# Order of DVE's, ScalarE's and TensorE's work in a fused group norm and attention kernel, changed around V and the output

## The chip, the cores and the metric

One core of one Trainium2 chip. The time is device microseconds of one execution; the runs shown are three executions of the whole program.

## What is computed

For each of 16 batch elements x of 512 channels by 1024 pixels (float32):

```
h = group_norm(x, 32 groups) * w + b
q, k, v = split(qkv_w @ h + qkv_b)              # 512 channels each
attn = softmax(q^T k / sqrt(512), over keys)    # 1024 x 1024
out = x + out_w @ (attn @ v^T)^T + out_b
```

## The kernel before, in words

The weights are multiplied together once: G from those of q and k, U from those of v and out. An element then has four stages on TensorE: T = G^T h (8 units, each a tile of 128 x 512 in one of the 8 PSUM banks), the score stage (7 products of half size by a Strassen-like scheme, with 4 tiles each, 28 units), V = h^T U (8 units, one for each tile of 128 keys), and the output (two halves of 512 queries, 4 tiles of 128 channels each, 8 units). Scores are held with keys in partitions.

Every matmul operand is split in a high part (rounded to fp32r by ScalarE) and a low part (what is left, by DVE), and each product is three matmuls: high by high, high by low, low by high (`three`, lines 262 to 264). So a T or V unit has 12 matmuls, a score unit 6 and an output unit 24, all of 512 columns: 96 + 168 + 96 + 192 = 552 per element.

Each engine runs its own written-out list and meets the others through semaphores.

- **TensorE** (lines 402 to 407): `t_units`, `score_products`, `v_units`, `output_units(b, 0)`, `output_units(b, 1)`. `t_bank_free` (308) holds a T unit until the scaled output has been read out of its bank: unit j of the next element waits for scaled tile j of this one. `t_bank_read` (321) holds a score product until what lies in its bank has been read.
- **ScalarE** (524 to 588): high parts of T (`t_direct_part`, `t_sum_part`), copies of scores, exponentials (510), high parts of the probabilities p (517) and of V (522), then the next element's h (425, 421) and the high parts of combined h (430).
- **DVE** (928 to 1029): low parts of T (816) and sums of T units (833, 839), sums of scores (846), the running maximum (858), statistics of the next x (690), subtraction of the maximum (865), low parts of V (875) and p (870), the tree that adds p over keys (881 to 887), the inverse of the sums (894), low part of the next h (724), its four combined sums (739 to 744) and their low parts (748), the key dot (757, 760), and the scaled output tiles (902), for which there are three buffers.
- **GpSimd** (650 to 665): maximum over partitions (631), twice; the group norm's power -1/2 (656); sum over partitions (636), twice; the adds of the scaled tiles into DRAM (645); the reduction of the key dot (623) between those of the two halves.
- **SP** (237 to 252) issues the other DMAs in a fixed order: x out and in, group statistics, then for half 0 the row of sums to DRAM and back in another shape, the inverses to DRAM and back to all partitions, the same for half 1, and the key bias. The transfers of one half are finished before those of the next begin, so the row of half 1 follows the inverses of half 0.

Group statistics (`group_variance`, `group_spread`, `affine_pair`) of element b + 1 are worked out during element b. `h_combined` (727) waits until both rows of sums are in DRAM, since it writes over the tiles they come from.

Of the kernel before, what the change touches and what calls it, by code (L numbers as in the profile page):

```python
# [37 lines left out]
T_SUM = {S1: (1, 2), S2: (3, 5), S3: (4, 6), S4: (7, 8)}  # L38

# [3 lines left out]
def attention_kernel(nc, x, wq, wk, wv, wo_t, cols, block_avg, out):  # L43
# [5 lines left out]
    with ctx:  # L49
# [80 lines left out]
        def t_bank(b, j):  # L130
            return (j + 1) % 8 if b == 0 else j
# [127 lines left out]
        def _(pe):  # L259
# [48 lines left out]
            def t_bank_free(b, j):  # L308
# [3 lines left out]
                elif j < 3:  # L312
                    pe.wait_ge(s_prod_lo[0], CT)
                elif j < 6:
                    pe.wait_ge(s_prod_lo[1], j - 2)
                elif j == 6:
                    pe.wait_ge(s_vec_sb, 3)
                else:
                    pe.wait_ge(s_prod_lo[1], CT)
# [25 lines left out]
            def score_products(b):  # L345
                for p, (a, name) in enumerate(PRODUCTS):
                    own_bank = p in (P_A12, P_S1, P_S4)
                    for i in range(CT):
                        cs = slice(i * P, (i + 1) * P)
                        if i == 0:  # L350
                            pe.wait_ge(s_tlo, b * 14 + 2 * a + 2)
# [36 lines left out]
            def output_units(b, nb):  # L388
                for c in range(CT):
                    cs = slice(c * P, (c + 1) * P)  # L390
                    pe.wait_ge(s_vlo, b * 8 + CT * nb + c + 1)
                    for m in range(MT):
                        if c == 0:
                            if nb == 0:
                                pe.wait_ge(s_vlo, b * 8 + m + 1)
                            pe.wait_ge(s_plo, b * 8 + nb * CT + m // 2 + 1)
                        a = three(ring[:, CT * nb + c, :], v_part(v_hi_all, m)[:, cs], v_part(v_lo_all, m)[:, cs],
                                  p_tiles(r_hi, nb, m)[:, 0, :], p_tiles(r_lo, nb, m)[:, 0, :], m == 0, m == MT - 1)
                    a.then_inc(s_unit, 1)

            v_hi_all, v_lo_all = r_hi, r_lo
# [8 lines left out]
        def _(act):  # L410
# [82 lines left out]

            def copy_scores(b, p, i, m, to, done):

                act.wait_ge(s_unit, b * UNITS + S0 + 4 * p + i + 1)
# [27 lines left out]
            for b in range(B):  # L524
                copy_a21(b, 0)
                copy_a21(b, 1)
                for kk in range(2):
                    t_direct_part(b, A22, kk)
                for kk in range(2):
                    t_sum_part(b, S1, kk)  # L530
                for kk in range(2):
                    t_direct_part(b, A11, kk)
                for a in (S2, S3):
                    for kk in range(2):
                        t_sum_part(b, a, kk)
                for kk in range(2):
                    t_direct_part(b, A12, kk)
                for kk in range(2):
                    t_sum_part(b, S4, kk)
# [514 lines left out]
```

## Time and profile before

| | before |
|---|---|
| median of 3 runs | 2242.78 us (2241.51 to 2244.41) |
| the profiled execution | 2240.99 us, span 2239.2 us |
| busy: PE, DVE, ACT, POOL | 2089.9, 1619.2, 953.3, 415.6 us |
| chain that ended last | PE 68%, DVE 16%, issue 6%, ACT 6%, POOL 2% |
| mean granted clock of TensorE | 0.961 of full speed |

PE is TensorE, ACT is ScalarE, POOL is GpSimd. Matmuls overlap in the records: each shows 0.39 us at full clock, but they start every 0.23 us, so the time between starts is the one to count with. The bracket behind a row gives the idle time of the engine before it and the last thing it waited for. "ring" is the PSUM tensor of 8 banks; "r_hi" and "r_lo" hold parts of T, V, p and combined h; "run_max" and "spare" also serve as buffers of scaled output.

### The profile page before, as it was taken

Reading aid. Unit: us, or ns where it says so; the run is one execution under the profiler, and the core shown is the slowest. Engines: PE = TensorE matmul, PEld = TensorE weight load, DVE = VectorE, ACT = ScalarE, POOL = GpSimd, SP = SyncE. Lnnn points to the kernel's source line nnn. Section 1 sums busy time; section 2 is a strip of 40 time slices with the busy share of each in tenths; the row PEclk is TensorE's granted clock in tenths of the full one; section 3 lists DMA queues with packets and bytes.
Section 4 is the critical chain, followed back from the end, with each engine's and each line's share of the span. In section 5 each row is a group of like instructions: output and inputs, shape, how many; then the busy total and the mean of one; then the engine's idle time right before and its main releaser. Section 6 shows DMA issues by size and latency. Waiting matters only on the chain.

```text
span 2239.2 us, 23037 instructions
## 1 busy us (share of the span) xinstructions
PE 2089.9 (93%) x8956; PEld 1712.7 (76%) x8956; DVE 1619.2 (72%) x1949; ACT 953.3 (43%) x1179; POOL 415.6 (19%) x237
## 2 busy tenths in 40 slices
PE   8789999898998989989899898989989899898998
PEld 6668778686886868868687786878868688686886
DVE  7678677776767678676776867767777776767754
ACT  6353344434444343444433445334453444444341
POOL 2012030211302113030120302203021130211302
PEclk9899999999999999999999999999999999999999
DMA  5204122140321303213031220402214032130303
GB/s 156 77 5 78 42 43 81 16 108 1 48 77 27 98 1 48 77 29 95 1 56 68 38 86 6 96 23 44 81 20 104 1 48 76 29 95 1 48 38 48
DMA packets 88269, 118.37 MB, mean 53 GB/s; under 512 B 47824, under 2 KB 48432, under 8 KB 88160
## 3 DMA queue, kind: packets, MB, share of 16 engines
q0 software_dynamic: 19296, 35.92, 11.4%
q1 hardware_dynamic: 68864, 80.98, 11.0%
q8 instruction: 71, 1.16, 0.2%
q14 instruction: 38, 0.31, 0.0%
HBM read 46.78 MB, written 67.74 MB: 51 GB/s over the span
## 4 chain that ended last, share of the span: by engine, by line
PE 68%; DVE 16%; issue 6%; ACT 6%; POOL 2%; POOLq 0%; DVEq 0%
PE ring L262 23%; PE ring L263 23%; PE ring L264 23%; DVE stage L865 3%; ACT stage L510 3%; DVE r_lo L875 2%; DVE stage L846 2%; DVE run_max L858 2%; DVE r_lo L870 2%; DVE stage L881 2%; ACT r_hi L517 2%; POOL all_max L631 1%; ACT r_hi L522 1%; DVE stage L884 1%; DVE group_mv L908 1%
## 5 line engine op out<-in xcount | busy, mean ns | idle before, releaser
L262 PE MATMUL ring<-r_hi 128*128 128x512 f32 x1568 | 636.5, 406 | 128.7 <-DVE r_lo L875 120.0
L263 PE MATMUL ring<-r_lo,r_hi 128*128 128x512 f32 x1568 | 629.7, 402 | 0.0
L264 PE MATMUL ring<-r_hi,r_lo 128*128 128x512 f32 x1568 | 628.6, 401 | 0.0
L262 PEld LDWEIGHTS ring<-r_hi 128*128 128x128 f32 x1568 | 306.5, 195 | 210.7 <-DVE r_lo L875 137.5
L264 PEld LDWEIGHTS ring<-r_hi,r_lo 128*128 128x128 f32 x1568 | 306.1, 195 | 66.2
L263 PEld LDWEIGHTS ring<-r_lo,r_hi 128*128 128x128 f32 x1568 | 306.9, 196 | 63.0
L510 ACT ACTIVATE stage<-stage 128x1024 f32<-128x1024 f32 x128 | 135.5, 1058 | 450.3 <-DVE stage L865 448.5
L497 ACT ACTIVATE stage<-ring,keybias 128x512 f32<-128x512 f32 x256 | 173.0, 688 | 248.7 <-PE ring L264 248.7
L631 POOL PARTITION_ALL_REDUCE all_max<-run_max x32 | 57.2, 1787 | 943.8 <-DVE run_max L858 668.7
L846 DVE TENSOR_TENSOR stage<-stage,ring 128x512 f32<-128x512 f32 x192 | 131.5, 685 | 115.4 <-PE ring L264 62.6
L262 PE MATMUL ring<-h_hi,g_hi 128*128 128x512 f32 x512 | 199.4, 389 | 0.0
L264 PE MATMUL ring<-h_hi,g_lo 128*128 128x512 f32 x512 | 199.2, 389 | 0.0
L264 PE MATMUL ring<-u_hi,h_lo 128*128 128x512 f32 x512 | 199.2, 389 | 0.0
L263 PE MATMUL ring<-h_lo,g_hi 128*128 128x512 f32 x512 | 199.2, 389 | 0.0
L263 PE MATMUL ring<-u_lo,h_hi 128*128 128x512 f32 x512 | 199.2, 389 | 0.0
L262 PE MATMUL ring<-u_hi,h_hi 128*128 128x512 f32 x512 | 199.2, 389 | 0.0
L636 POOL PARTITION_ALL_REDUCE stage<-stage x32 | 129.8, 4056 | 340.6 <-DVE stage L887 180.7
L865 DVE TENSOR_TENSOR stage<-stage,all_max 128x1024 f32<-128x1024 f32 x128 | 183.3, 1451 | 0.0
L875 DVE TENSOR_TENSOR r_lo<-ring,r_hi 128x512 fp32r<-128x512 f32 x128 | 86.6, 687 | 116.8 <-ACT r_hi L522 116.8
L870 DVE TENSOR_TENSOR r_lo<-stage,r_hi 128x1024 fp32r<-128x1024 f32 x128 | 155.9, 1218 | 16.7 <-ACT r_hi L517 16.7
L858 DVE TENSOR_TENSOR run_max<-run_max,stage 128x512 f32<-128x512 f32 x192 | 137.8, 722 | 36.4 <-ACT stage L497 32.0
L262 PE MATMUL ring<-h_hi,r_hi 128*128 128x512 f32 x384 | 150.3, 391 | 14.7 <-DVE stage L833 14.7
(100 smaller groups left out, 3012.5 us busy)
## 6 DMA issues: line engine op xcount, KB each, us to landing
xs<-x_in SPq DMA_DIRECT2D x64, 512.0 KB, 6.0
out<-xs SPq DMA_DIRECT2D x64, 512.0 KB, 3.2
out<-run_max POOLq DMA_DIRECT2D x86, 256.0 KB, 4.3
out<-spare POOLq DMA_DIRECT2D x42, 256.0 KB, 4.5
inv<-inv_row SPq DMA_DIRECT2D x32, 256.0 KB, 3.8
stage<-stage POOLq DMA_DIRECT2D x3, 512.0 KB, 8.5
stage<-wk SPq DMA_DIRECT2D x4, 256.0 KB, 4.0
stage<-wq SPq DMA_DIRECT2D x4, 256.0 KB, 5.1
```

Source lines behind the costliest of these rows:

```text
L262: nc.tensor.matmul(ps_out, st_hi, m_hi, start=first, stop=False, skip_group_check=goes_on)
L263: nc.tensor.matmul(ps_out, st_hi, m_lo, start=False, stop=False, skip_group_check=goes_on)
L264: return nc.tensor.matmul(ps_out, st_lo, m_hi, start=False, stop=last, skip_group_check=goes_on)
L497: nc.scalar.activation(stage[:, to, :], ring[:, i, :], ACT.Identity, bias=keybias[:, m:m + 1]).then_inc(done, 1)
L510: nc.scalar.activation(here, here, ACT.Exp, scale=SCALE).then_inc(s_exp, 1)
L631: nc.gpsimd.partition_all_reduce(all_max[:, :], run_max[nb][:, :], P, bass.bass_isa.ReduceOp.max).then_inc(s_allmax, 1)
L636: nc.gpsimd.partition_all_reduce(stage[:, 8 * nb + 1, :], stage[:, 8 * nb, :], P, bass.bass_isa.ReduceOp.add).then_inc(s_allsum, 1)
L846: nc.vector.tensor_tensor(stage[:, to, :], stage[:, to, :], ring[:, CT + i, :], ALU.add).then_inc(done, 1)
L858: nc.vector.tensor_tensor(run_max[nb][:, :], first, stage[:, 8 * nb + m, :], ALU.max).then_inc(s_rmax[nb], 1)
L865: nc.vector.tensor_tensor(here, here, all_max[:, :].rearrange("p (o n) -> p o n", o=1).to_broadcast([P, 2, HALF]), ALU.subtract).then_inc( ...
L870: nc.vector.tensor_tensor(p_tiles(r_lo, nb, 2 * q, 2), stage[:, 8 * nb + 2 * q:8 * nb + 2 * q + 2, :], p_tiles(r_hi, nb, 2 * q, 2).bitcast ...
L875: nc.vector.tensor_tensor(v_part(r_lo, m), ring[:, m, :], v_part(r_hi, m).bitcast(FP32), ALU.subtract).then_inc(s_vlo, 1)
```

## The change

- Output: `output_units` walks over key tiles outside and the four channel tiles inside, so that the four banks of a half fill together (but for the last half of the last element, which keeps the old order). V's low part m and the pair m // 2 of p are waited for at each key tile.
- T and scores: ScalarE and DVE split A22 and A11 first, then A12, and the sums S1 to S4 last; `T_SPLIT` holds the new counts that TensorE waits for. The first copies of scores don't add the key bias; `add_first` on DVE adds it, and the key bias is computed later.
- Around V: group variance before the S4 sums; V's low parts 5 to 7 and the subtractions of half 1 ahead of the group spread and of the sum tree of half 0; low parts of h, combined h, key dot and scaled tiles in new places.
- First element: other banks for T units 3 to 7, the low parts of combined h before the key dot, another order of splits.

```diff
+T_SPLIT = {A22: 0, A11: 2, A12: 4, S1: 6, S2: 8, S3: 10, S4: 12}
...
         def t_bank(b, j):
-            return (j + 1) % 8 if b == 0 else j
+            return (1, 2, 3, 4, 0, 5, 6, 7)[j] if b == 0 else j
...
-                elif j < 6:
-                    pe.wait_ge(s_prod_lo[1], j - 2)
-                elif j == 6:
+                elif j < 7:
+                    pe.wait_ge(s_prod_lo[1], (1, CT, 2, 3)[j - 3])
+                else:
                     pe.wait_ge(s_vec_sb, 3)
-                else:
-                    pe.wait_ge(s_prod_lo[1], CT)
...
-                            pe.wait_ge(s_tlo, b * 14 + 2 * a + 2)
+                            pe.wait_ge(s_tlo, b * 14 + T_SPLIT[a] + 2)
...
             def output_units(b, nb):
-                for c in range(CT):
+                by_keys = (b, nb) != (B - 1, NB - 1)
+                steps = [(c, m) for m in range(MT) for c in range(CT)]
+                if not by_keys:
+                    steps.sort()
+                for c, m in steps:
                     cs = slice(c * P, (c + 1) * P)
-                    pe.wait_ge(s_vlo, b * 8 + CT * nb + c + 1)
-                    for m in range(MT):
-                        if c == 0:
-                            if nb == 0:
-                                pe.wait_ge(s_vlo, b * 8 + m + 1)
-                            pe.wait_ge(s_plo, b * 8 + nb * CT + m // 2 + 1)
...
-                    a.then_inc(s_unit, 1)
+                    if m == 0 and (c == 0 or nb == 0):
+                        pe.wait_ge(s_vlo, b * 8 + CT * nb + c + 1)
+                    if c == 0:
+                        pe.wait_ge(s_vlo, b * 8 + m + 1)
+                        pe.wait_ge(s_plo, b * 8 + nb * CT + m // 2 + 1)
+                    a = three(...)
+                    if m == MT - 1:
+                        a.then_inc(s_unit, 1)
...
# ScalarE
+            def copy_first(b, i):
+                act.wait_ge(s_bias_out, (b + 1) * DMA)
+                act.wait_ge(s_unit, b * UNITS + S0 + 4 * P_A11 + i + 1)
+                nc.scalar.activation(stage[:, i, :], ring[:, i, :], ACT.Identity).then_inc(s_p1, 1)
...
-                copy_a21(b, 0)
-                copy_a21(b, 1)
+                if b > 0:
+                    for kk in range(2):
+                        copy_a21(b, kk)
+                for a in (A22, A11):
+                    for kk in range(2):
+                        t_direct_part(b, a, kk)
+                if b == 0:
+                    for kk in range(2):
+                        copy_a21(b, kk)
                 for kk in range(2):
-                    t_direct_part(b, A22, kk)
-                for kk in range(2):
-                    t_sum_part(b, S1, kk)
-                for kk in range(2):
-                    t_direct_part(b, A11, kk)
-                for a in (S2, S3):
+                    t_direct_part(b, A12, kk)
+                for a in (S1, S2, S3, S4):
                     for kk in range(2):
                         t_sum_part(b, a, kk)
-                for kk in range(2):
-                    t_direct_part(b, A12, kk)
-                for kk in range(2):
-                    t_sum_part(b, S4, kk)
-                act.wait_ge(s_kb, b + 1)
                 for i in range(CT):
-                    copy_scores(b, P_A11, i, i, i, s_p1)
+                    copy_first(b, i)
...
-                exponential(b, 1, 0)
-                p_part(b, 1, 0)
-                v_hi_part(b, 6)
-                v_hi_part(b, 7)
-                for q in range(1, CT):
+                for q in range(2):
                     exponential(b, 1, q)
                     p_part(b, 1, q)
+                v_hi_part(b, 6)
+                exponential(b, 1, 2)
+                p_part(b, 1, 2)
+                v_hi_part(b, 7)
+                exponential(b, 1, 3)
+                p_part(b, 1, 3)
...
# DVE
             h_combined(0)
+            for c in range(CT):
+                h_combined_rest(0, c)
...
-            for c in range(CT):
-                h_combined_rest(0, c)
-            dve.wait_ge(s_bqk, 1)
...
+            def add_first(b, i):
+                if i == 0:
+                    dve.wait_ge(s_kb, b + 1)
+                dve.wait_ge(s_p1, b * 4 + i + 1)
+                dve.wait_ge(s_unit, b * UNITS + S0 + 4 * P_A12 + i + 1)
+                nc.vector.scalar_tensor_tensor(stage[:, i, :], ring[:, CT + i, :], keybias[:, i:i + 1], stage[:, i, :],
+                                               ALU.add, ALU.add).then_inc(s_c11, 1)
...
+                if b == 0:
+                    for a in (A22, A11):
+                        for kk in range(2):
+                            t_direct_rest(b, a, kk)
                 for kk in range(2):
-                    t_direct_rest(b, A22, kk)
+                    if b > 0:
+                        t_direct_rest(b, A22, kk)
                     t_sum(b, S1, kk)
                 if b > 0:
                     scale_output(b - 1, 1, 3)
                 for kk in range(2):
-                    t_sum_rest(b, S1, kk)
-                for kk in range(2):
-                    t_direct_rest(b, A11, kk)
+                    if b > 0:
+                        t_direct_rest(b, A11, kk)
                     t_sum(b, S2, kk)
                     t_sum(b, S3, kk)
-                for a in (S2, S3):
-                    for kk in range(2):
-                        t_sum_rest(b, a, kk)
-                key_bias(b)
                 for kk in range(2):
                     t_direct_rest(b, A12, kk)
                     t_sum(b, S4, kk)
-                for kk in range(2):
-                    t_sum_rest(b, S4, kk)
-
+                for a in (S1, S2, S3, S4):
+                    for kk in range(2):
+                        t_sum_rest(b, a, kk)
+                key_bias(b)
                 for i in range(CT):
-                    add_scores(b, P_A12, i, i, s_p1, s_c11)
+                    add_first(b, i)
...
+                if more:
+                    group_variance(b + 1)
                 for i in range(CT):
                     add_scores(b, P_S4, i, 8 + i, s_p2, s_c12)
...
                 v_rest(b, 4)
+                subtract_max(b, 1, 0)
+                subtract_max(b, 1, 1)
+                v_rest(b, 5)
+                subtract_max(b, 1, 2)
+                subtract_max(b, 1, 3)
+                v_rest(b, 6)
+                p_rest(b, 1, 0)
+                v_rest(b, 7)
                 if more:
                     group_spread(b + 1)
                 sum_tree(b, 0)
-                v_rest(b, 5)
-                subtract_max(b, 1, 0)
-                subtract_max(b, 1, 1)
-                v_rest(b, 6)
-                v_rest(b, 7)
+                p_rest(b, 1, 1)
+                p_rest(b, 1, 2)
+                p_rest(b, 1, 3)
                 if more:
                     affine_pair(b + 1)
-                p_rest(b, 1, 0)
-                subtract_max(b, 1, 2)
-                p_rest(b, 1, 1)
-                subtract_max(b, 1, 3)
-                p_rest(b, 1, 2)
-                p_rest(b, 1, 3)
                 sum_tree(b, 1)
+
+                if more:
+                    for k in range(CT - 1):
+                        h_rest(b + 1, k)
                 inverse(b, 0)
-
                 if more:
-                    h_rest(b + 1, 0)
-                scale_output(b, 0, 0)
-                if more:
-                    h_rest(b + 1, 1)
-                scale_output(b, 0, 1)
-                if more:
-                    h_rest(b + 1, 2)
                     h_rest(b + 1, 3)
-                scale_output(b, 0, 2)
+                    h_combined(b + 1)
+                for c in range(CT):
+                    scale_output(b, 0, c)
                 inverse(b, 1)
-                if more:
-                    h_combined(b + 1)
-                scale_output(b, 0, 3)
                 if more:
                     for k in range(CT):
                         key_dot(b + 1, k)
-                scale_output(b, 1, 0)
-                if more:
-                    h_combined_rest(b + 1, 0)
-                    h_combined_rest(b + 1, 1)
-                scale_output(b, 1, 1)
-                if more:
-                    h_combined_rest(b + 1, 2)
-                    h_combined_rest(b + 1, 3)
-                scale_output(b, 1, 2)
+                    for c in range(CT):
+                        h_combined_rest(b + 1, c)
+                for c in range(CT - 1):
+                    scale_output(b, 1, c)
```

The wait of `copy_scores` for the key bias moved into the function, and `key_bias(0)` now waits for the dot of the two biases itself.

## Rows read from the trace of the kernel before

**Rows 1.** Who waited for whom on TensorE: total us, times, longest.

```profile
PE ring L262 <- DVE r_lo L875: 120.0, 31, 5.3
```

**Rows 2.** TensorE in order of time: start us, us, line, operation, idle before.

```profile
73.39 0.77 PE L262 MATMUL ring<-h_hi,r_hi 128*128 128x512 f32 x1 [14.68 <-DVE stage L833]
...
900.00 0.39 PE L262 MATMUL ring<-h_hi,r_hi 128*128 128x512 f32 x1
...
944.20 0.39 PE L262 MATMUL ring<-u_hi,h_hi 128*128 128x512 f32 x1
...
1097.91 0.80 PE L262 MATMUL ring<-r_hi 128*128 128x512 f32 x1 [4.63 <-DVE r_lo L875]
...
2232.89 0.39 PE L264 MATMUL ring<-r_hi,r_lo 128*128 128x512 f32 x1
```

**Rows 3.** Stretches: us, busy (x) by engine, granted clock, DMA, GB/s.

```profile
1093.30:1096.90 3.60, 0.00 (x0) 0.00 (x0) 3.53 (x3) 0.00 (x0) 0.00 (x0) 1.00 0.09 2
1097.40:1107.60 10.20, 6.81 (x15) 4.93 (x16) 8.57 (x10) 5.09 (x6) 4.15 (x1) 0.50 0.01 2
```

**Rows 4.** DVE in order of time, around V and the output.

```profile
1070.92 2.34 DVE L865 TENSOR_TENSOR stage<-stage,all_max 128x1024 f32<-128x1024 f32 x2
...
1088.39 0.68 DVE L875 TENSOR_TENSOR r_lo<-ring,r_hi 128x512 fp32r<-128x512 f32 x1
1092.84 0.17 DVE L916 COPY group_pair<-group_mv 32x16 f32<-32x16 f32 x1 [3.77 <-POOL group_rstd L656]
...
1097.18 0.68 DVE L875 TENSOR_TENSOR r_lo<-ring,r_hi 128x512 fp32r<-128x512 f32 x1
```

**Rows 5.** ScalarE in order of time: one exponential and the next.

```profile
1099.03 1.06 ACT L510 ACTIVATE stage<-stage 128x1024 f32<-128x1024 f32 x1 [11.73 <-DVE stage L865]
...
1102.03 1.06 ACT L510 ACTIVATE stage<-stage 128x1024 f32<-128x1024 f32 x1
```

**Rows 6.** GpSimd in order of time.

```profile
1092.22 0.59 POOL L656 TENSOR_TENSOR group_rstd<-group_veps,minus_half 32x1 f32<-32x1 f32 x1 [7.04 <-issue]
1103.45 4.24 POOL L636 PARTITION_ALL_REDUCE stage<-stage  x1 [10.64 <-issue]
```

**Rows 7.** DVE in order of time, beside reductions of GpSimd.

```profile
51.13 8.96 DVE L748 TENSOR_TENSOR r_lo<-stage,r_hi 128x1024 fp32r<-128x1024 f32 x4
...
1104.49 3.26 DVE L865 TENSOR_TENSOR stage<-stage,all_max 128x1024 f32<-128x1024 f32 x1
```

**Rows 8.** SP's queue in order of time: the DMAs it issued.

```profile
981.79 0.34 SPq L230 DMA_DIRECT2D inv_row<-own_inv  x1
983.24 0.32 SPq L235 DMA_DIRECT2D inv<-inv_row  x1
985.99 0.24 SPq L224 DMA_DIRECT2D sum_row<-stage  x1
987.15 0.32 SPq L226 DMA_DIRECT2D own_sum<-sum_row  x1
```

**Rows 9.** DVE in order of time: next h, scaled tiles; last, the page's DMA line.

```profile
987.23 0.69 DVE L902 TENSOR_TENSOR run_max<-ring,inv 128x512 f32<-128x512 f32 x1 [4.36 <-DMA inv<-inv_row]
...
997.18 0.68 DVE L902 TENSOR_TENSOR run_max<-ring,inv 128x512 f32<-128x512 f32 x1
...
1002.40 0.68 DVE L902 TENSOR_TENSOR run_max<-ring,inv 128x512 f32<-128x512 f32 x1
...
2209.53 1.29 DVE L902 TENSOR_TENSOR run_max<-ring,inv 128x512 f32<-128x512 f32 x2 [5.58 <-DMA inv<-inv_row]
...
2215.93 0.69 DVE L902 TENSOR_TENSOR run_max<-ring,inv 128x512 f32<-128x512 f32 x1 [4.43 <-DMA out<-run_max]
...
out<-run_max POOLq DMA_DIRECT2D x86, 256.0 KB, 4.3
```

**Rows 10.** DVE in order of time, in the first element.

```profile
44.70 1.22 DVE L744 TENSOR_TENSOR stage<-stage 128x1024 f32<-128x1024 f32 x1
...
64.69 1.40 DVE L833 SCALAR_TENSOR_TENSOR stage<-ring,t_bias,stage 128x512 f32<-128x512 f32 x2
```

## What the change was predicted to do

> **What bounds the kernel now.** I read first who waits for whom on TensorE, then TensorE in order of time, the granted clock by stretches, and last the other engines in one period. TensorE waits in one place only: 31 waits, 120.0 us in all, for a low part of V [rows 1]. Elsewhere it issues a 512-column matmul every 0.2267 us (195 steps, 900.00 to 944.20) [rows 2]. An element of the batch has 552 of them (96 for T, 168 scores, 96 V, 192 output), 125.1 us; by the sum below it costs 11.2 us more.
>
> I count from A, the start of the output stage. The stalled matmul starts at 1097.91; its forerunner started 4.63 + 0.39 earlier, at 1092.89 [rows 2], and is the last of five key tiles (15 matmuls), so A = 1089.72. Here output tile 0 walks through eight key tiles in 5.4 us, and DVE can't keep up: it stood 3.77 us until the group's root arrived, and then ran the spread and sum tree (4.3 us, 1092.84 to 1097.18) ahead of V's part 5 [rows 4]. With 31 waits in 16 elements there is a second one for the parts behind it. The idle also halves the clock: 1.00 through 1093.3 to 1096.9, then 0.50, the 1.2 GHz level, for 10.2 us [rows 3]. Both waits and the slow stretch make up the 11.2 us.
>
> **Part 1, output by key tiles.** Now all four tiles advance with the key tile, 12 matmuls or 2.72 us each, so V part m is due at A + 2.72 m, and probabilities' pair q at A + 5.44 q. Part 7 is due at A + 19.0 instead of A + 4.8. The matmuls and weight loads are as many as before; only banks alternate every three matmuls. The score products in the 195 steps change banks every six matmuls, some 20 times, and the mean step doesn't show it to 0.1 us in all, so a change costs under 0.005. I take 0 (bounds: 0 and 0.5 us for the 112 changes more of an element).
>
> **Part 2, DVE and ScalarE around A.** The group variance (about 1.1 us) goes ahead of the S4 sums, where DVE waits for TensorE, so the subtractions, at A - 18.8 before [rows 4], start 0.4 us earlier. V's part 4, A - 1.3 before, starts at A - 1.8. From start to start an operation on 1024 columns takes 1.14 us and one on 512 takes 0.60, a little less than the records of 1.22 and 0.68 (the two subtractions of rows 4 take 2.34, one record more than one step). Two subtractions, part 5, two subtractions end at A + 4.0. ScalarE gets its first subtraction at A + 0.05; an exponential, a copy and two V copies take 3.0 us together [rows 5], so V's high part 7 comes at A + 6.7, its low part at A + 7.3 to 7.9. It is due at 19.0: **the old stall is gone**, with 11 us to spare. All p parts of half 1, due from A + 21.8, are also in time (below).
>
> **Part 3, what is late next.** Everything pushed behind V now stands in one DVE queue up to the first scaled tile of half 1, which frees a bank for T unit 4 of the next element: due at A + 43.52 + 4 x 2.72 = A + 54.4. Step by step:
> - Group spread 0.16, sum tree of half 0 4.18: A + 12.2. Three low parts of p, 3.4.
> - GpSimd's sum over partitions starts 11.2 us after the root, with no wait that the profile shows (1092.22 to 1103.45), A + 13.3 to 14.0, until about A + 17.9 [rows 6]. An operation of 1024 columns under it took 3.26 instead of 1.21 [rows 7]: +2.05. Affine 0.46, sum tree 4.18: A + 22.35.
> - h low parts 0 to 2: 3 x 1.14, and +2.05 for GpSimd's second sum, which used to run while DVE waited for a DMA: A + 27.8 (28.5 if ScalarE's copies, which wait for the first sum's row in DRAM, are the slower).
> - The inverse of half 0 stands there. The combined h sums wait for the second sum's row in DRAM, and SP sends that only behind the inverse's two transfers: 0.2 to the store, 1.45 to the load, 0.35 to issue it, 1.16 to land [rows 8], so A + 31.0 to 31.7, one to two us later than DVE (h low part 3 done at 29.1 to 29.9). **A new wait.** The four sums take 4.65, 1.14 each and 0.1 for their own order [rows 10]: A + 35.7 to 36.4. The inverses land 4.0 after their issue (983.24 to 987.23) [rows 8, 9], before that.
> - Four scaled tiles now stand together, and there are three buffers. The fourth waits until the first one's add into DRAM has landed. The end of the kernel shows exactly that: 2209.53 to 2215.93, 6.4 us from the first to the fourth [rows 9]. A + 42.1 to 42.8. **The second new wait.** Behind it are queued the other inverse, the key dot and all four low parts of combined h.
> - 0.7 for it and the inverse, 4.6 for the key dot (997.78, behind 997.18, to 1002.40) [rows 9]: A + 47.4 to 48.1. Four low parts under GpSimd's key-dot reduction took 8.96 in the first element, 4.6 alone [rows 7]; it is four again, together: A + 56.3 to 57.0. The scaled tile needs 0.69 more.
>
> So bank 4 is free at A + 57.0 to 57.7, against 54.4: **2.6 to 3.3 us of stall per element, 2.9 taken.** Bounds: with the median landing of such a store, 4.3 us from an issue 1.3 us behind the tile [rows 9], the fourth tile comes 0.8 earlier; with that and one hold of 2.05 fewer the stall is 0.05. One hold more, or the stores slower by as much, makes it 4.5 to 5. I take the middle, since three stores close together are what the end's row has. T units 5 to 7 are served in time: the last scaled tile of half 1 ends at A + 63.9 and is due at A + 65.5.
>
> Would such a stall halve the clock? After 3.6 us of idle the clock was still 1.00 [rows 3]. I take 2.9 us as too short, and the cost of the slow stretch as zero.
>
> **Part 4, T and score stage.** A11's products need two splits ahead of them instead of three; sums' low parts come last. DVE has 8 x 0.6 us of these left when A12's unit is split, ends about S + 7 (S is the start of the score stage), and they are due from S + 10.9. Key bias and first sums follow the product of A12, which they have to wait for. Input shift, its DMAs and the statistics move by under 1 us, and the statistics end before the add at S + 23.8 that was next. Nothing on TensorE's path: 0, with the due times as cover.
>
> **Part 5, start.** In the first element bank 0 was the last one freed, and TensorE stood 14.68 us until 73.39 [rows 2]. Now bank 0 holds T unit 4, and needs the fourth sum only. DVE: combined h done at 44.70 + 1.14, four low parts 4.56, key dot 4.63, bias 0.08: 55.1. Four splits and four sums at 0.66 (two in 1.40) [rows 10]: the fourth sum ends at 60.4, TensorE starts at 60.6. **12.8 us earlier**, and with 2.2 us of idle, without the slow matmuls after it. These eight run beside GpSimd's key-dot reduction; they read PSUM. Bounds: 0, and the 4.4 us that the low parts lost to it [rows 7]. I take 0, since the 1024-column rows that were held all read SBUF alone.
>
> **The sum.** First score matmul 60.6; from it to the end 16 x 552 - 96 = 8736 matmuls x 0.2267 = 1980.2; from the last matmul's slot (2232.89 + 0.23) [rows 2] to the end 6.1, as before; 15 stalls x 2.9 = 43.5. Span 2090.4. The same sum for the kernel before, 73.4 + 1980.2 + 6.1 = 2059.7, leaves 179.5 for 16 stalls with their slow stretches, 11.2 each. The profiled execution took 1.8 more than its span, and the median 1.8 more than that: **2094**, 6.6% less than 2242.8 (2090.4 + 3.6).
>
> **Rivals.**
> - *No new stall* (0.22). DVE reaches bank 4 before A + 54.4 because the stores land faster, or a hold falls between operations. 2046.9 + 3.6 = 2050.5. For: the median landing is shorter than my row. Against: it needs 2.6 us in a chain where I gave no reserve. Between it and mine each us of stall is 15 us.
> - *The clock falls at the new stall* (0.12). A stall over about 3.7 us, or a chip less patient than rows 3 show, makes the matmuls behind it run at 0.50 for 10.2 us, 5.1 us lost: 2094 + 15 x 5.1 = 2170. The Trainium skill ("TensorE: Matmul & The Clock Gate", HAM oscillation) says that a wait in every round can slow the clock every round, which rows 3 agree with for the old stall.
> - *Slower than before* (0.03). Place: the three reductions of GpSimd that DVE's queue in part 3 now meets. If each held DVE until its own end, and PSUM's readers too, the low parts of p would wait from A + 13.4 to A + 17.9 (2.4 us more than I count), h's low part 1 1 us more and combined h's 1.7 more: a stall of 8.0, the clock falls, 5.1 more, and the start loses 4.4: 2046.9 + 4.4 + 15 x 13.1 + 3.6 = 2251. From a stall of 6.1 on the element costs more than the 11.2 before. Against: the operation that began 1.04 us into a reduction of 4.24 lost 2.05, and not the 3.2 that were left of it [rows 6, 7]. The Trainium skill ("SBUF — State Buffer", Who interferes with whom) holds for that case that the later one "fully blocks" until the first is done, if it reads two tensors of SBUF; the length of the hold in rows 7 doesn't agree with it.
> - *It does not do what it says* (0.03): TensorE still stops in the output stage, as DVE's queue has something ahead of V's last parts that I missed: 2242.8, less the start's 12.8 at most.
>
> **How the numbers follow.** Mine (stall 1.5 to 4.5, no slow clock) has 0.60 and spans 2073 to 2118. The range takes it, the first rival below and a little above: 2048 to 2125; outside are the others, 0.18. A measurement of this kernel can tell about 0.2% from no change. Faster: 0.60 + 0.22 + 0.12 = 0.94; same 0.02 and slower 0.04 from the last two, the second of them split.
>
> **What would show it.** TensorE's waits: none for V's low parts; 15 of about 2.9 us, before matmuls that read h and g, for a scaled tile (line of the output scaling). DVE waiting 2 to 4 us for a store of the output, and shortly for a sum's row. A granted clock of 1.00 from the first score matmul on. First score matmul near 60.6. It is wrong if TensorE's waits are absent, fall elsewhere, or carry 0.50 behind them.

## The result and the profile after

The changed kernel takes 2205.4 us (median of 4 runs, 2198.7 to 2214.4) against 2242.2 for the kernel before: ratio 0.984, 95% interval 0.980 to 0.988. It is faster, by 1.6% where 6.6% were forecast, and far outside the range of 2048 to 2125. Its profiled execution took 2198.66 us, with a span of 2196.8.

Who waits for whom on TensorE, in the changed kernel (line numbers of that kernel: 924 is the scaled output tile, 846 a sum of T units; total, times, longest):

```profile
PE ring L263 <- DVE run_max L924: 74.6, 10, 8.3
PE ring L263 <- DVE spare L924: 39.3, 5, 8.4
...
PE ring L263 <- DVE stage L846: 1.9, 1, 1.9
```

The 31 waits for V's low parts [rows 1] are gone, all of them. In their place stand the 15 waits for a scaled tile that the prediction named, but they take 113.9 us: 7.6 each and not 2.9. TensorE in order of time shows both ends of the argument, the start and one stall:

```profile
60.01 0.47 PE L263 MATMUL ring<-h_hi,r_hi 128*128 128x512 f32 x1 [1.88 <-DVE stage L846]
...
1128.15 0.79 PE L263 MATMUL ring<-h_hi,g_hi 128*128 128x512 f32 x1 [7.42 <-DVE run_max L924]
```

The first score matmul starts at 60.0 (60.6 forecast, 73.4 before [rows 2]). With the prediction's own sum, 60.0 + 1980.2 + 6.1 = 2046.3 is the span without stalls, so 150.5 us, 10.0 a stall, go with the 15 stalls. 7.6 of it is waiting; the other 2.4 is, above all, slow matmuls. The stretches around this stall (columns as in [rows 3]):

```profile
1121.00:1123.50 2.50, 0.00 (x0) 0.00 (x0) 2.50 (x1) 0.45 (x1) 2.50 (x1) 1.00 0.14 54
...
1128.10:1131.00 2.90, 2.85 (x7) 2.27 (x8) 2.90 (x5) 0.00 (x0) 2.54 (x3) 0.50 0.60 60
...
1134.00:1139.00 5.00, 5.00 (x23) 4.13 (x22) 4.14 (x7) 1.38 (x2) 0.86 (x1) 1.00 0.66 95
```

The clock is at 1.00 in the first microseconds of the idle, at 0.50 (1.2 GHz) when the matmuls come back, and at 1.00 again some microseconds later, as before the change behind the old stall.

The stalled matmul starts 7.81 after its forerunner, so T unit 4 was due at 1120.57 and, 54.4 earlier, A = 1066.17. DVE from V's last part on, to be held against part 3 of the prediction:

```profile
1073.55 0.69 DVE L897 TENSOR_TENSOR r_lo<-ring,r_hi 128x512 fp32r<-128x512 f32 x1 [0.70 <-ACT r_hi L534]
...
1074.31 2.27 DVE L903 TENSOR_TENSOR stage<-stage 128x2048 f32<-128x2048 f32 x1
...
1077.88 0.69 DVE L909 TENSOR_TENSOR stage<-stage 128x512 f32<-128x512 f32 x1
1078.49 3.48 DVE L892 TENSOR_TENSOR r_lo<-stage,r_hi 128x1024 fp32r<-128x1024 f32 x3
...
1084.68 3.29 DVE L906 TENSOR_TENSOR stage<-stage 128x1024 f32<-128x1024 f32 x1
...
1091.62 1.23 DVE L736 TENSOR_TENSOR h_lo<-stage,h_hi 128x1024 fp32r<-128x1024 f32 x1 [2.93 <-ACT h_hi L426]
...
1097.30 0.17 DVE L916 RECIPROCAL own_inv<-own_sum 128x4 f32<-128x4 f32 x1
...
1103.22 1.23 DVE L751 TENSOR_TENSOR stage<-stage 128x1024 f32<-128x1024 f32 x1 [3.57 <-DMA sum_row<-stage]
...
1107.89 0.68 DVE L924 TENSOR_TENSOR spare<-ring,inv 128x512 f32<-128x512 f32 x1
...
1113.24 0.69 DVE L924 TENSOR_TENSOR spare<-ring,inv 128x512 f32<-128x512 f32 x1 [3.47 <-DMA out<-spare]
...
1118.54 8.96 DVE L760 TENSOR_TENSOR r_lo<-stage,r_hi 128x1024 fp32r<-128x1024 f32 x4
1127.42 1.27 DVE L924 TENSOR_TENSOR run_max<-ring,inv 128x512 f32<-128x512 f32 x2
```

| step, us behind A | forecast | measured |
|---|---|---|
| V's low part 7 starts | 7.3 | 7.4 |
| first sum tree done | 12.2 | 12.4 |
| GpSimd's first sum starts | 13.3 to 14.0 | 18.5 |
| second sum tree done | 22.35 | 22.5 |
| inverse of half 0 | 27.8 to 28.5 | 31.1 |
| combined h starts | 31.0 to 31.7 | 37.05 |
| first scaled tile | 35.7 to 36.4 | 41.7 |
| fourth scaled tile | 42.1 to 42.8 | 47.1 |
| first scaled tile of half 1 | 56.3 to 57.0 | 61.25 |

Both new waits are there, with the 3.57 and 3.47 us in brackets. Both sum trees and all before them are right to 0.2 us, the second one partly by luck: the hold of 2.05 us by GpSimd's sum, forecast on the low parts of p, fell on the second tree (3.29 in its row, for some 1.2). GpSimd's sum is the first step that is off. GpSimd and SP in the same stretch:

```profile
1067.93 1.67 POOL L668 TENSOR_TENSOR group_rstd<-group_veps,minus_half 32x1 f32<-32x1 f32 x1 [6.67 <-issue]
1084.64 3.25 POOL L648 PARTITION_ALL_REDUCE stage<-stage  x1 [15.04 <-DVE stage L903]
1088.90 3.23 POOL L648 PARTITION_ALL_REDUCE stage<-stage  x1 [1.01 <-DVE stage L909]
```

```profile
1097.50 0.34 SPq L231 DMA_DIRECT2D inv_row<-own_inv  x1
1100.10 0.32 SPq L236 DMA_DIRECT2D inv<-inv_row  x1
1100.47 0.29 SPq L225 DMA_DIRECT2D sum_row<-stage  x1
1103.21 0.32 SPq L227 DMA_DIRECT2D own_sum<-sum_row  x1
```

The sum starts 16.7 us after the start of the root, where it was 11.2 before [rows 6]. What both kernels have in common is the sum tree: it ended at 1078.57 here, 6.1 us before the sum starts. Before, the operation ahead of V's part 5 (start 1097.18 [rows 4]) was the tree's last, and the sum followed at 1103.45 [rows 6], 6.2 us after the tree's end. It is so in all of the first 15 elements: 6.0 to 6.4 us from the tree to the sum before, 5.9 to 6.5 after, while from the root it is 11.0 to 11.4 before and 15.9 to 16.8 after. The last element has no root ahead of its sum, as no next x needs one, and already in the kernel before its sum starts 0.2 us after the tree (DVE, then GpSimd):

```profile
2183.37 0.69 DVE L887 TENSOR_TENSOR stage<-stage 128x512 f32<-128x512 f32 x1
```

```profile
2184.26 3.23 POOL L636 PARTITION_ALL_REDUCE stage<-stage  x1 [8.28 <-DVE stage L887]
```

And the store of half 1's row, 0.37 us behind the load of the inverses, took 2.74 us to land instead of 1.16 [rows 8], counted to SP's next issue.

### The profile page after: what moved, and what is told of

It is laid out like the page before. It is cut to its first block, busy times and chain, and to the rows that moved or that the text cites. A ratio compares the mean times of both kernels' runs of the same rounds, so it can differ in the third digit from the quotient of the medians.

```text
span 2196.8 us, 23374 instructions
## 1 busy us (share of the span) xinstructions
PE 2065.0 (94%) x8956; PEld 1700.9 (77%) x8956; DVE 1618.8 (74%) x1949; ACT 935.1 (43%) x1179; POOL 424.3 (19%) x237
## 3 DMA queue, kind: packets, MB, share of 16 engines
q8 instruction: 71, 1.16, 0.2%
## 4 chain that ended last, share of the span: by engine, by line
PE 42%; DVE 27%; ACT 13%; DMA 7%; issue 7%; POOL 2%; SPq 0%; DVEq 0%; ACTq 0%; POOLq 0%
PE ring L263 14%; PE ring L264 14%; PE ring L265 14%; DVE r_lo L892 4%; ACT stage L522 4%; DVE r_lo L760 4%; DVE stage L887 3%; DMA sum_row<-stage 3%; ACT r_hi L529 3%; DVE stage L903 2%; DVE r_lo L897 2%; POOL stage L648 2%; ACT stage L430 2%; ACT h_hi L426 2%; DMA out<-run_max 2%
## 5 line engine op out<-in xcount | busy, mean ns | idle before, releaser
L263 PE MATMUL ring<-r_hi 128*128 128x512 f32 x1568 | 611.6, 390 | 8.1 <-DVE r_lo L690 8.1
L264 PE MATMUL ring<-r_lo,r_hi 128*128 128x512 f32 x1568 | 611.0, 390 | 0.0
L265 PE MATMUL ring<-r_hi,r_lo 128*128 128x512 f32 x1568 | 610.8, 390 | 0.0
L264 PEld LDWEIGHTS ring<-r_lo,r_hi 128*128 128x128 f32 x1568 | 294.9, 188 | 60.9
L263 PE MATMUL ring<-h_hi,g_hi 128*128 128x512 f32 x512 | 214.7, 419 | 113.9 <-DVE run_max L924 74.6
L643 POOL PARTITION_ALL_REDUCE all_max<-run_max x32 | 57.2, 1788 | 920.6 <-DVE run_max L880 651.9
L509 ACT ACTIVATE stage<-ring,keybias 128x512 f32<-128x512 f32 x192 | 132.2, 688 | 227.6 <-PE ring L265 227.6
L263 PEld LDWEIGHTS ring<-h_hi,g_hi 128*128 128x128 f32 x512 | 103.9, 203 | 142.4 <-DVE run_max L924 78.8
L492 ACT ACTIVATE r_hi<-ring,t_bias 128x512 fp32r<-128x512 f32 x96 | 65.1, 690 | 278.0 <-PE ring L265 278.0
L430 ACT ACTIVATE stage<-xs,h_bias,h_scale 128x1024 f32<-128x1024 f32 x62 | 76.5, 1234 | 216.9 <-DMA sum_row<-stage 213.3
L648 POOL PARTITION_ALL_REDUCE stage<-stage x32 | 113.0, 3555 | 256.1 <-DVE stage L903 167.2
L880 DVE TENSOR_TENSOR run_max<-run_max,stage 128x512 f32<-128x512 f32 x192 | 132.5, 695 | 36.4 <-ACT stage L509 32.0
```

Source lines behind the costliest of these rows:

```text
L263: nc.tensor.matmul(ps_out, st_hi, m_hi, start=first, stop=False, skip_group_check=goes_on)
L264: nc.tensor.matmul(ps_out, st_hi, m_lo, start=False, stop=False, skip_group_check=goes_on)
L265: return nc.tensor.matmul(ps_out, st_lo, m_hi, start=False, stop=last, skip_group_check=goes_on)
L430: nc.scalar.activation(h_full[:, k, :], xs[:, k, :], ACT.Identity, bias=h_bias[:, k:k + 1], scale=h_scale[:, k:k + 1]).then_inc(done, 1)
L509: nc.scalar.activation(stage[:, to, :], ring[:, i, :], ACT.Identity, bias=keybias[:, m:m + 1]).then_inc(done, 1)
L648: nc.gpsimd.partition_all_reduce(stage[:, 8 * nb + 1, :], stage[:, 8 * nb, :], P, bass.bass_isa.ReduceOp.add).then_inc(s_allsum, 1)
```

## The experiments

**The output order alone.** The kernel before with only `output_units` exchanged for the new one:

```diff
-                for c in range(CT):
-                    pe.wait_ge(s_vlo, b * 8 + CT * nb + c + 1)
-                    for m in range(MT):
+                by_keys = (b, nb) != (B - 1, NB - 1)
+                steps = [(c, m) for m in range(MT) for c in range(CT)]
+                if not by_keys:
+                    steps.sort()
+                for c, m in steps:
...
```

> The kernel before with the output walked by key tiles and nothing else of the change. Theory (what the output order gains is real, and what costs time in the changed kernel is DVE's new order behind V): the 31 waits for V's low parts vanish; first score matmul stays near 73.4 us; TensorE's next waits are short ones (about 0.6, 1.7 and 1.3 us an element) for scaled tile 3 and for the splits of T, as the old order of T's splits is tight; some 2060 us without them, 2105 us with them, clock near 1.00. Rival (the walk by key tiles itself costs TensorE, through its bank changes or its waits): time near 2200 us, with steps between output matmuls longer than 0.2267 us.

Measured: 2094.9 us, ratio 0.934 (0.933 to 0.936), clock 0.996. TensorE's waits there (908 is the scaled tile, 822 a low part of T, 839 the sum in the first element):

```profile
PE ring L262 <- DVE stage L839: 14.7, 1, 14.7
PE ring L262 <- DVE r_lo L822: 12.0, 15, 0.8
...
PE ring L262 <- DVE run_max L908: 0.8, 4, 0.2
PE ring L262 <- DVE spare L908: 0.6, 3, 0.2
```

This one part brings 6.6%, four times what the whole change brings. The walk by key tiles costs nothing that shows; DVE's old order is just fast enough for it. The time lies between the 2060 and the 2105 of the expectation, as the waits were shorter than I had worked out.

**SP's store of half 1's row first**, in the changed kernel:

```diff
+                send_sums(b, 0)
                 own_sums(b, 0)
+                send_sums(b, 1)
                 spread_inverses(b, 0)
                 own_sums(b, 1)
```

(`send_sums` is the wait for the sum and the store of its row, taken out of `own_sums`.)

> The changed kernel, with SP's store of the sums' row of half 1 ahead of the two transfers of the inverses of half 0. Theory: DVE's wait of 3.6 us before the combined sums of h goes, and each stall at T unit 4 shrinks by 3 to 3.6 us, from 7.6 to about 4.2; with part of the slow clock gone too, some 2140 to 2155 us. Rival (the stall is set elsewhere, for instance by the store that the fourth scaled tile waits for): the wait moves to the next in DVE's queue and the time stays within 0.5% of 2205 us.

Measured: 2155.3 us, ratio 0.962 (0.958 to 0.965). SP's queue:

```profile
1068.34 0.22 SPq L225 DMA_DIRECT2D sum_row<-stage  x1
1074.68 0.34 SPq L233 DMA_DIRECT2D inv_row<-own_inv  x1
1077.32 0.34 SPq L238 DMA_DIRECT2D inv<-inv_row  x1
```

The row leaves 6.3 us before the inverse, DVE no longer waits for it, and TensorE's 15 waits come to 66.1 us, 4.4 each: 3.2 less. The theory holds, at the upper end of its time.

**GpSimd without the root**, in the changed kernel. It leaves out the power -1/2 (DVE puts 1/(variance + eps) in its place), so the values of h are others; the work is the same:

```diff
-                if b + 1 < B:
-                    pool.wait_ge(s_gstep, b * GSTEP + 2)
-                    nc.gpsimd.tensor_tensor(group_rstd[:, :], group_veps[:, :], minus_half[0:GROUPS, 0:1],
-                                            ALU.pow).then_inc(s_grstd, 1)
...
+                dve.wait_ge(s_gstep, (n - 1) * GSTEP + 2)
+                nc.vector.reciprocal(group_rstd[:, :], group_veps[:, :]).then_inc(s_grstd, 1)
```

> The changed kernel, with the group's power -1/2 on GpSimd left out: DVE takes 1/(variance + eps) in its place, which changes the values, not the amount of the other work. Theory: in both kernels GpSimd starts its first sum over partitions 6.1 us after DVE's sum tree has ended (1097.3 to 1103.5 before, 1078.6 to 1084.6 after), because it changes its program after the root, and only once the tree's semaphore has come; without the root the sum starts 0.3 us after the tree, the next h starts 4.5 to 5 us earlier on ScalarE, the stall shrinks by 3.5 to 5 us, to 3 to 4 us; 2130 to 2155 us. Rival (the sum starts a fixed 11 to 15 us after the root or is late for another reason): it still starts 6 us after the tree and the time stays near 2205 us.

Measured: 2142.9 us, ratio 0.956 (0.954 to 0.957). GpSimd's first sum and the DVE operations around it:

```profile
921.31 4.03 POOL L648 PARTITION_ALL_REDUCE stage<-stage  x1 [17.70 <-DVE stage L905]
```

```profile
920.42 0.69 DVE L905 TENSOR_TENSOR stage<-stage 128x512 f32<-128x512 f32 x1
921.03 5.54 DVE L888 TENSOR_TENSOR r_lo<-stage,r_hi 128x1024 fp32r<-128x1024 f32 x3
```

The sum starts 0.2 us after the tree and not 6.1, and the hold of 2.06 us now falls on the low parts of p (5.54 instead of 3.48), where I had put it. The stalls are 3.8 us. So the 6.1 us need the root ahead of the sum, and by the rows of both kernels above they begin only when the tree has ended. What GpSimd does in them no row shows; the change of program that the expectation speaks of stays a guess.

**DVE's old tail**, in the changed kernel, everything else as changed (the edit is condensed: several calls stand on a line, and the lines `if more:` are left out):

```diff
                 sum_tree(b, 1)
-                for k in range(CT - 1): h_rest(b + 1, k)
                 inverse(b, 0)
-                h_rest(b + 1, 3); h_combined(b + 1)
-                for c in range(CT): scale_output(b, 0, c)
+                h_rest(b + 1, 0); scale_output(b, 0, 0)
+                h_rest(b + 1, 1); scale_output(b, 0, 1)
+                h_rest(b + 1, 2); h_rest(b + 1, 3); scale_output(b, 0, 2)
                 inverse(b, 1)
-                for k in range(CT): key_dot(b + 1, k)
-                for c in range(CT): h_combined_rest(b + 1, c)
-                for c in range(CT - 1): scale_output(b, 1, c)
+                h_combined(b + 1); scale_output(b, 0, 3)
+                for k in range(CT): key_dot(b + 1, k)
+                scale_output(b, 1, 0)
+                h_combined_rest(b + 1, 0); h_combined_rest(b + 1, 1); scale_output(b, 1, 1)
+                h_combined_rest(b + 1, 2); h_combined_rest(b + 1, 3); scale_output(b, 1, 2)
```

> The changed kernel, with DVE's order from the second sum tree to the last scaled tile as in the kernel before (inverse first, scaled tiles in between the low parts of h and the key dot, the first scaled tile of half 1 ahead of the low parts of combined h). Theory: the first scaled tile of half 1 ends 46 to 49 us behind the start of the output stage, where T unit 4 needs it at 54.4, so TensorE has no wait behind 60 us; clock 1.00; span 2046 us, time about 2050 us. Rival (the stall comes from the work moved behind V in general, not from the order of this tail): stalls of over 3 us stay at T unit 4, time over 2120 us.

Measured: 2049.2 us (2048.2 to 2051.2), ratio 0.914 (0.913 to 0.915). Its page, and one stretch over nearly all of it:

```profile
PE 2033.0 (99%) x8956; PEld 1682.6 (82%) x8956; DVE 1607.7 (78%) x1949; ACT 940.3 (46%) x1179; POOL 403.7 (20%) x237
...
100.00:2040.00 1940.00, 1940.00 (x8560) 1606.94 (x8559) 1531.73 (x1835) 883.80 (x1104) 385.23 (x219) 1.00 0.24 54
```

TensorE has no wait behind the first score matmul and never leaves full clock. GpSimd's 6.1 us and SP's slow store are still in this kernel (its first sums have 14.9 to 15.5 us of idle ahead of them, and the row of half 1 takes 2.3 to 3.7 us to land). They cost nothing, as nothing on TensorE's way stands behind them. It is the version that beats both, by 8.6% and 7.1% (2049.2 of 2205.4).

**Tile by tile again**, in the changed kernel and in the one with the old tail; the edit is `by_keys = False` in both.

> The changed kernel with the output walked tile by tile again. Theory (DVE's queue behind V sets when T unit 4 starts, whatever TensorE does in between): TensorE waits some 3.3 us in the output stage for V's parts 6 and 7 (low part 7 comes 7.4 to 8.1 us behind the stage's start, due at 4.8), and the stall at T unit 4 is that much shorter, about 4.3 instead of 7.6; the sum per element stays 7.6 and the time within 1.2% of 2205 us, 2180 to 2210. Rival (the walk by key tiles is what brought the gain): the old stalls add to the new, and the time goes to 2250 us or more.

> The kernel of the run with DVE's old tail, 2049 us, with the output walked tile by tile again. Theory: with no stall at T unit 4 to hide it, the wait for V's parts 6 and 7 shows in full, 3.3 us for each of 16 elements, in two waits of under 3 us, without a fall of the clock: 2049 + 53 = some 2102 us. Rival (V's new place in DVE's list is enough, the walk is not needed): 2049 to 2060 us.

Measured: 2181.4 us (0.973, 0.971 to 0.976), faster than the change itself, and 2121.4 us (0.946, 0.945 to 0.948). TensorE's waits in the first of them (897 is V's low part):

```profile
PE ring L263 <- DVE r_lo L897: 46.0, 32, 1.6
PE ring L263 <- DVE run_max L924: 23.7, 10, 3.4
...
PE ring L263 <- DVE spare L924: 8.3, 5, 3.1
```

2.9 us an element at V's parts and 2.1 at the scaled tile: 5.0 in all, where the expectation had 3.3 and 4.3 and the 7.6 of the changed kernel kept. The time fell into its range for another reason, the clock. The span of 2181.4 is 135.1 above the 2046.3 without stalls; 78.0 of that are these waits, and the other 57.1, 3.6 an element, are above all slow matmuls, more than the 2.4 of the changed kernel. Two short waits were enough for it:

```profile
1067.51 0.50 PE L263 MATMUL ring<-r_hi 128*128 128x512 f32 x1 [1.37 <-DVE r_lo L897]
...
1070.03 0.80 PE L263 MATMUL ring<-r_hi 128*128 128x512 f32 x1 [1.54 <-DVE r_lo L897]
...
1123.52 0.50 PE L263 MATMUL ring<-h_hi,g_hi 128*128 128x512 f32 x1 [0.93 <-DVE run_max L924]
```

```profile
1070.00:1075.00 5.00, 4.97 (x12) 3.96 (x13) 4.93 (x6) 1.25 (x2) 0.00 (x0) 0.50 0.06 2
```

Slow matmuls bring TensorE later to T unit 4, so that less of a stall is left there: 0.93 us in this element, and 2.8 to 3.4 in the five in which the clock stayed at 1.00 behind V's waits. In this kernel the walk by key tiles only makes one long stall out of two or three short ones. With the old tail nothing hides V's waits, and the same 2.9 us (46.1 over 16) come back as 4.5 us an element (72.3 us over 16), the rest again slow matmuls: the mean clock is 0.990 instead of 0.998, and it fell behind V's waits in 8 of the 16 elements, which I had not expected. 2102 was forecast.

**The key dot ahead of the fourth scaled tile**, in the changed kernel, and this together with SP's store first:

```diff
-                for c in range(CT):
+                for c in range(CT - 1):
                     scale_output(b, 0, c)
-                inverse(b, 1)
                 if more:
                     for k in range(CT):
                         key_dot(b + 1, k)
+                scale_output(b, 0, CT - 1)
+                inverse(b, 1)
+                if more:
...
```

> The changed kernel with the key dot moved ahead of the fourth scaled tile of half 0. Theory: DVE's wait for the first tile's add into DRAM (3.5 to 3.7 us) is filled with the 4.6 us of the dot, the first scaled tile of half 1 and the stall at T unit 4 come 2.9 to 3.6 us earlier; 7.6 becomes 4.0 to 4.7, and 2145 to 2160 us. Rival (GpSimd's queue: its key-dot reduction stands behind the fourth tile's add, which now comes later): the reduction starts later, its hold still falls into DVE's low parts, and the gain is under 1 us an element, over 2185 us.

> Both edits together: SP's store of half 1's row first, and the key dot ahead of the fourth scaled tile. Theory: the two gains add up (3.2 and 2.9 to 3.6 us), 0.8 to 1.5 us of stall are left at T unit 4, and as the idle is short TensorE's clock stays at 1.00, so the 2.5 us of slow matmuls behind each stall go too: 2060 to 2072 us. Rival (the clock falls at any such wait): 2090 us or more with a clock of 0.98.

Measured: 2148.2 us (0.957, 0.956 to 0.959) with stalls of 4.4 us (66.3 over 15), and 2074.5 us (0.926, 0.924 to 0.928), with stalls of 0.85 (12.7 over 15); the second is 2.5 us above its expected range. DVE in the second kernel (928 is the scaled tile, 773 the start of the key dot):

```profile
920.37 0.68 DVE L928 TENSOR_TENSOR spare<-ring,inv 128x512 f32<-128x512 f32 x1
920.97 0.77 DVE L773 TENSOR_SCALAR stage<-stage,k_dir 128x1024 f32<-128x1024 f32 x1
...
925.62 0.69 DVE L928 TENSOR_TENSOR run_max<-ring,inv 128x512 f32<-128x512 f32 x1
```

The dot fills the wait for the buffer. The gains of the waits add up: 3.2 + 3.2 = 6.4 by the single edits, 6.7 together. Of the times: 50.1 and 57.2 us for each alone, 130.9 together, so 23.6 more than their sum. 5.8 us of that are the waits; the rest goes with the slow clock: the mean clock is 0.979 with either edit alone and 0.997 with both. A stretch right behind a wait of 1.76 us there:

```profile
936.30:946.30 10.00, 10.00 (x44) 8.29 (x45) 9.20 (x15) 2.07 (x3) 3.55 (x4) 1.00 0.79 105
```

**The old order of T's splits**, in the kernel with the old tail, for all elements but the first:

```diff
-T_SPLIT = {A22: 0, A11: 2, A12: 4, S1: 6, S2: 8, S3: 10, S4: 12}
+T_FIRST = {A22: 0, A11: 2, A12: 4, S1: 6, S2: 8, S3: 10, S4: 12}
+def t_split(b, a):
+    return T_FIRST[a] if b == 0 else 2 * a
...
```

> The kernel of 2049 us (key tiles and DVE's old tail) with the order of T's splits and sums as in the kernel before, for every element but the first. Theory: without other waits the old order shows, as it did with the key tiles alone (15 waits of 0.8 us for the low parts of T, and 0.8 us more an element in steps of TensorE too short to be listed as waits): 1.6 us an element, 2070 to 2078 us. Rival (the order of the splits is hidden, as the prediction had it): 2047 to 2052 us.

Measured: 2049.8 us (0.914, 0.913 to 0.916), no difference from 2049.2. My expectation was wrong and the prediction's part 4 right: that order is hidden. So the short waits for T's low parts with the output order alone don't come from that order by itself. DVE stands nowhere in that run from 934.4 to 971.0, around such a wait at 962.6: it comes late to T from the work ahead. Which of the other differences takes these waits away was not run apart.

## Why the prediction was wrong, and where it was right

Right: the old stall goes by the walk and by V's new place; the new stall stands at T unit 4, behind the row of half 1 and behind the fourth scaled tile; the start is 12.8 us earlier (13.4 measured, with 1.88 us of idle for 2.2); the T and score stage costs nothing (the last run); bank changes cost nothing (8560 matmuls in the 1940 us stretch, 0.2266 each). Splits and sums of T that read PSUM were not held by GpSimd's reduction in the first element, as the third rival would have had it. DVE and GpSimd there:

```profile
54.52 2.72 DVE L829 SCALAR_TENSOR_TENSOR r_lo<-ring,t_bias,r_hi 128x512 fp32r<-128x512 f32 x4
57.15 4.03 DVE L846 SCALAR_TENSOR_TENSOR stage<-ring,t_bias,stage 128x512 f32<-128x512 f32 x6
```

```profile
54.74 6.14 POOL L635 PARTITION_ALL_REDUCE stage<-stage  x1 [4.14 <-DVE stage L772]
```

Ten operations at 0.66 us each beside a reduction of 6.14. The Trainium skill ("SBUF — State Buffer", Who interferes with whom) says that a DVE instruction with at most one SBUF input does not contend with GpSimd. These ten, which read one tensor of SBUF beside PSUM and a column of biases, agree with it.

Wrong was the size of one term, the stall, 2.9 forecast and 7.6 measured. By the table it came in three pieces:

- **The step that failed first** is "GpSimd's sum over partitions starts 11.2 us after the root". I read one gap with no named wait as a fixed time from the root. It is 6.1 us from the end of DVE's tree, and the root ahead is only the condition for it. Moving the tree away from the root, which the change does, was exactly what told the two readings apart; the last element of the kernel before could have told them apart beforehand. The sum started 4.5 to 5.2 us later than forecast, ScalarE's copies of the next h behind it, and the inverse 2.6 to 3.3 us later. The run without the root takes 3.8 us off the stall.
- **"1.16 to land"** for half 1's row came from a store issued 2.75 us behind the load that spreads the inverses [rows 8]. Issued 0.37 us behind it, it took 2.74 here and 3.2 in the element shown of the run without the root; the inverse's own store took 2.60 for 1.45 in this element, and 2.50 in the same element before. That the nearness to the load is what slows the store fits all elements, but no run varied it alone. With these, combined h starts 5.4 to 6.1 us late instead of 2.6 to 3.3. The run with the row first takes 3.2 off the stall.
- The wait for the fourth tile was 1.05 us shorter than its row (5.35 for 6.4), and brought 5.7 down to 4.6. It is real all the same: filling it took 3.2 off.

**The slow clock** is the second term, 2.4 us an element for the 0 forecast. It stood in the second rival, with 0.12, for a stall over some 3.7 us, and at 7.6 that was met. The prediction's "2.9 us as too short" was not safe either: in the changed kernel walked tile by tile a stall of 2.81 at T unit 4 has 0.50 behind it.

```profile
1656.17 0.80 PE L263 MATMUL ring<-h_hi,g_hi 128*128 128x512 f32 x1 [2.81 <-DVE spare L924]
```

```profile
1656.20:1658.20 2.00, 2.00 (x5) 1.63 (x6) 2.00 (x4) 0.00 (x0) 1.62 (x3) 0.50 0.40 17
```

The rival's 5.1 us was twice too much, as about half of the slow stretch falls into the idle. Five microseconds of error in a stall became 7 in the element: (7.6 - 2.9) + 2.4 = 7.1, times 15 = 107, and 2094 + 107 = 2201 of the measured 2205.

I had called the chain one "where I gave no reserve", and gave the range 0 to 4.5 us of stall on such a base. A chain of a dozen steps over four engines, laid out anew, needed a wider upper end.

## What to carry to other kernels

A gap that the profile calls issue has a start, and one place in the trace can't tell whether it counts from the instruction ahead of it or from the wait behind it; look for a second place where the two differ before moving one of them. Here it was the last element, which has no root. Work taken off a critical spot comes to rest in front of the next deadline of the same queue: here one part of the change brought 6.6%, the rest of the change took three quarters of it back, and with the old order of DVE's tail the whole comes to 8.6%. When four tiles go through three buffers, put the next long operation ahead of the fourth.

## What the runs showed of the hardware that I had not expected

- GpSimd's first sum over partitions starts 5.9 to 6.5 us after its input is ready if a power operation stands before it in its list (15 elements of each kernel), and 0.2 us after it without one. The time is spent after the wait and not in the idle before.
- The 2 KB store of a row of sums takes 1.1 us to SP's next issue when it is alone, as for half 0, and 2.5 to 3.6 us in the changed kernel's first 15 elements, where it is issued 0.37 us behind the load that spreads one row over all partitions (256 KB written).
- The clock had not fallen behind waits of 1.76 us in the run with both edits, and it had behind 7.42. Between these the single wait doesn't decide: with DVE's old tail, walked tile by tile, two waits of 1.4 and 1.5 us three matmuls apart had 0.50 behind them in 8 elements and 1.00 in 7 others. Where a wait of 3.8 us is the rule (the run without the root) an element loses (2141.0 - 2046.3) / 15 = 6.3, 2.5 us more than the wait.
